# Five chained attentions on one core: key copies issued by GpSimd instead of SyncE, and fewer, wider products in the local attention

## What is computed

```
x = L0(x, ctx)   # masked self-attention, layer norm, masked cross-attention, layer norm, MLP, layer norm
x = L1(x, ctx)   # qn + attention(qn, layer_norm(ctx))
x = L2(x, ctx)   # local attention: key j is kept when i - 64 <= j < i + 65; one key head for all 16 query heads; gate, RMS norm
x = L3(x, ctx)   # attention on layer-normed inputs, then layer norm and a GELU MLP, two residuals
# every attention: softmax(scale * q k^T + mask) v
```

## Time and profile before

| | |
|---|---|
| time of three runs | 2371.82 us median (2369.3 to 2372.09) |
| span of the profiled execution | 2371.4 us |
| mean granted TensorE clock | 0.983 |
| busy: PE, PEld, DVE, ACT, POOL | 94%, 71%, 68%, 64%, 22% |

### The profile page before, as it was taken

One profiled execution on the slowest core, in us unless ns is written; L12 is line 12 of the kernel. 1 busy time (PEld: TensorE's weight loads), 2 busy tenths in 40 slices (PEclk: granted clock), 3 DMA queues, 4 the chain that ended last, 5 costly groups with the idle time before them and its releaser, 6 DMA issues.

```text
span 2371.4 us, 50835 instructions
## 1 busy us (share of the span) xinstructions
PE 2233.3 (94%) x18354; PEld 1675.2 (71%) x18354; DVE 1604.2 (68%) x3312; ACT 1509.9 (64%) x3167; POOL 527.9 (22%) x1120
## 2 busy tenths in 40 slices
PE   6999999999999999999999999999999999999966
PEld 3677777777776676877867677777778686776654
DVE  6768586776767577586675777677756767586422
ACT  5665756777565667658565777566676764766532
POOL 4311122331112132121212332121332212122100
PEclk9999999999999999999999999999999999999977
DMA  7512222331312133113022332112322321122100
GB/s 213 151 47 64 64 60 69 96 93 35 80 37 53 47 99 87 46 52 92 21 66 70 91 82 65 51 45 70 88 61 68 83 60 42 51 61 55 45 7 19
DMA packets 164247, 159.22 MB, mean 67 GB/s; under 512 B 17824, under 2 KB 162720, under 8 KB 162976
## 3 DMA queue, kind: packets, MB, share of 16 engines
q1 hardware_dynamic: 164000, 155.97, 24.0%
HBM read 35.71 MB, written 4.19 MB: 17 GB/s over the span
## 4 chain that ended last, share of the span: by engine, by line
PE 55%; issue 20%; DVE 10%; ACT 5%; POOL 3%; POOLq 2%; DVEq 2%; DMA 1%; SPq 1%; ACTq 0%
PE work L1147 14%; PE work L1138 11%; PE unit L1211 6%; PE unit L1182 5%; PE out L1235 5%; DVE neg_max L1026 5%; PE unit L1207 3%; PE work L1129 2%; ACT unit L792 2%; ACT probs L807 2%; PE unit L1202 2%; PE work L1351 2%; POOL resid L662 1%; DMA query_stack<-max_rows 1%; POOL rstd L652 1%
## 5 line engine op out<-in xcount | busy, mean ns | idle before, releaser
L1026 DVE TENSOR_REDUCE neg_max<-unit 128x2 f32<-128x512 f32 (+1 forms) x1280 | 766.5, 653 | 229.5 <-PE unit L1182 223.3
L807 ACT ACTIVATE probs<-unit 128x512 f32<-128x512 f32 (+1 forms) x1280 | 643.7, 580 | 254.8 <-PE unit L1211 251.9
L1147 PE MATMUL work<-par,hidden_t 128*128 128x256 f32 x1792 | 419.6, 384 | 6.9 <-ACT hidden_t L743 5.8
L1147 PEld LDWEIGHTS work<-par,hidden_t 128*128 128x128 f32 x1792 | 333.1, 191 | 58.0 <-ACT hidden_t L743 9.2
L1182 PE MATMUL unit<-key_stack,query_stack 96*128 96x256 bf16 x2048 | 321.6, 277 | 43.8 <-DMA query_stack<-query_pieces 10.4
L1211 PE MATMUL unit<-query_stack,key_stack 99*128 99x256 bf16 x2048 | 347.6, 275 | 6.9 <-DMA query_stack<-max_rows 3.6
L1138 PE MATMUL work<-tok_t,par 128*128 128x256 f32 x1408 | 339.2, 388 | 3.6 <-ACT tok_t L743 2.5
L1138 PEld LDWEIGHTS work<-tok_t,par 128*128 128x128 f32 x1408 | 260.7, 193 | 44.0 <-ACT tok_t L743 7.2
L1182 PEld LDWEIGHTS unit<-key_stack,query_stack 96*128 96x128 bf16 x2048 | 174.3, 98 | 160.3 <-ACT unit L792 57.0
L1235 PE MATMUL out<-probs,values 128*17 128x256 f32 x4096 | 258.4, 383 | 3.6 <-ACT hidden_t L818 3.4
L1211 PEld LDWEIGHTS unit<-query_stack,key_stack 99*128 99x128 bf16 x2048 | 191.7, 98 | 73.5 <-ACT probs L807 17.5
(11 more groups left out here) (164 smaller groups left out, 3235.8 us busy)
## 6 DMA issues: line engine op xcount, KB each, us to landing
query_stack<-query_pieces SPq DMA_DIRECT2D x480, 128.0 KB, 2.4
key_stack<-key_pieces SPq DMA_DIRECT2D x384, 128.0 KB, 2.4
tok_t<-in_x_features SPq DMA_DIRECT2D x16, 256.0 KB, 2.8
m_in<-in_mask_self SPq DMA_DIRECT2D x16, 256.0 KB, 3.0
x_in<-in_x SPq DMA_DIRECT2D x16, 256.0 KB, 3.0
c_in<-in_ctx SPq DMA_DIRECT2D x16, 256.0 KB, 2.9
ctx_t<-in_ctx_features SPq DMA_DIRECT2D x16, 256.0 KB, 2.9
m_in<-in_mask_cross SPq DMA_DIRECT2D x16, 256.0 KB, 3.1
```

Source lines behind the costliest of these rows:

```text
L807: a_.activation(probs[:, n % PROB_BUFS, k, :, 0:width(l)], bank[:, :, 0:width(l)], ACT.Exp, scale=SCALE[l]).then_inc(exped, 1)
L1026: v.tensor_reduce(neg_max[:, n % HALVES, t, 2 * (u % 4):2 * (u % 4) + 2], bank[:, :, 0:width(l)], AX.X, ALU.max, negate=True).then_inc(max ...
L1147: last = pe.matmul(bank[:, t, :], src[:, t * P:(t + 1) * P], weight, start=(n == 0), stop=(n == len(parts) - 1))
```

## The change

1. **Key copies.** ksplit's six DMAs become steps kcopy0, kcopy1 and kcopy2 (three, two and one DMAs) that POOL issues in its own order; qsplit's become qcopy steps, which stay on SP. The waits are the same ones, now on POOL's queue: for ACT's high piece and for the attention that last used the stack, then for each of DVE's two lower pieces. 480 DMAs move (384 of 128 KB, 96 of 8 KB).
2. **Flag-setting products.** `bits_read` looks up who next uses the bank. If it is a unit that PE starts itself, the flags are of no use and the 128-column product is left out. 18 of 256 remain.
3. **exp products of l2.** The two products of 192 columns become one of 384, since both heads share their weights.
4. **Small buffers.** The norms' moments rotate over 12 places and no longer 4 (`stats` over 2, `sumsq` and `var_eps` over 4), without new waits. The table that says which units ACT primes is written per unit now; all its entries are 1, as before.

The order string is new, but the instructions of DVE and ACT come in the same sequence as before, and those of PE too, except for the products that are gone or merged. On POOL, besides the inserted DMAs, one pair of norm instructions has another place. The core of the diff:

```
+        def copies(eng, key):
+            b, l, step = key
+            keys, piece = step[0] == "k", int(step[-1])
...
+            if piece == 0:
+                if last:
+                    eng.wait_ge(weighed, WEIGH_NO.upto(last + ("weigh3",)))
+                eng.wait_ge(high, no.upto(cut))
+            else:
+                eng.wait_ge(low, 2 * no.upto(cut) - (2 - piece))
+            for at, which in enumerate(rows):
+                if which != piece:
+                    continue
+                dst = stack_[at:ROWS:len(rows), :, :]
+                if keys and l == "l2":
+                    eng.dma_start(dst[:, 0, :], pieces[0:HD, piece, 0, :]).then_inc(placed, 16)
+                else:
+                    eng.dma_start(dst.rearrange("d h n -> d (h n)"),
+                                 pieces[:, piece].rearrange("p c n -> p (c n)")).then_inc(placed, 16)
...
-                    if step in ("ksplit", "qsplit"):
-                        split(key)
+                    if step[:5] == "qcopy":
+                        copies(sp, key)
...
+                    if step[:5] == "kcopy":
+                        copies(pool, key)
...
+        def bits_read(key, half):
+            n = T * UNIT_NO.place[key] + half
+            for m in range(n + UNIT_BUFS, T * len(UNIT_NO.keys), UNIT_BUFS):
+                b, l, step = UNIT_NO.keys[m // T]
+                of_prime = step[:3] in ("pre", "prx")
+                if l != "l2" or not of_prime:
+                    return of_prime
+            return False
...
-                        set_bits(bank[:, :, n:S], S - n)
+                        if bits_read(key, k):
+                            set_bits(bank[:, :, n:S], S - n)
...
-                    for i in range(2):
+                    if l == "l2":
+                        last = pe.matmul(bank[:, :, 0:n], keys[0:MAX_ROWS, 0, k * P:(k + 1) * P],
+                                         queries[0:MAX_ROWS, 2 * u:2 * u + 2, columns(l, k)],
+                                         start=False, stop=True, skip_group_check=True)
+                    for i in range(2 if l != "l2" else 0):
```

More of the change, by code:

```diff
@@ L164 @@
[L164 to L176 removed]
+    "0AA1AsAA0000s00000s1111BBQAA0Q0Q0Q1B011110QA0Q00sQ0Qs00AAAAA00000A0B00s0000s0BR1sR1R10R11sB0AR0001R1"
@@ new lines, with prime_steps, primes @@
+    "fffffPPPPfffdffffefffeffdefeedfffeefedfefefdffeeeedffdfeeddddfffefffffedefffeefeffefffffedeeffeffPPP"
+    "PPffffffffefffeffefeffeefffffefeleflflflfflflleffflefffffffffeffffffffffffffffffffffffffffffffffffff"
+    "fffffffffffffffffffffffff"
+)
+LANES = "0123456789abcdefABCDEFGHIJKLMNOPsQRSTUVWXYZghijkl"
+def prime_steps():
+    return [tuple(step.split(".")) for step in PRIMES.split()]
+def primes(b, l, step):
+    row = PRIMED.get((l, step[:3]))
+    return row is not None and row.split()[b][int(step[3:])] == "1"
@@ new lines, in runs @@
+def runs(key):
+    b, l, step = key
+    if step[:3] in ("pre", "prx"):
+        return primes(b, l, {"pre": "max", "prx": "exp"}[step[:3]] + step[3:])
+    return True
+def schedule():
+    lanes = [(b, steps) for steps in (chain_steps(), beside_steps()) for b in range(B)]
+    lanes += [(B, [("setup", step) for step in SETUP_STEPS])]
+    lanes += [(b, prime_steps()) for b in range(B)]
+    left = {c: (b, iter(steps)) for c, (b, steps) in zip(LANES, lanes)}
+    return [key for key in [(left[c][0],) + next(left[c][1]) for c in ORDER] if runs(key)]
@@ L207, with __init__ @@
 class Numbers:
-    def __init__(self, chosen):
-        self.keys = [k for k in SCHEDULE if chosen(k[1], k[2])]
+    def __init__(self, chosen, also=lambda key: True):
+        self.keys = [k for k in SCHEDULE if chosen(k[1], k[2]) and also(k)]
         self.place = {k: n for n, k in enumerate(self.keys)}
@@ L224 @@
 WORK_NO = Numbers(lambda l, step: step in THROUGH_WORK)
-UNIT_NO = Numbers(lambda l, step: step[:3] in ("pre", "prx") or step[:3] == "max" and l not in PRIMED_MAX
-                  or step[:3] == "exp" and l not in PRIMED_EXP)
+UNIT_NO = Numbers(lambda l, step: step[:3] in ("pre", "prx", "max", "exp"),
+                  lambda key: primer(key) is None)
+FIRST_MASKED = {}
+for _key in UNIT_NO.keys:
+    if _key[2][:3] == "max":
+        FIRST_MASKED.setdefault(_key[:2], _key)
 PRIME_NO = Numbers(lambda l, step: step[:3] in ("pre", "prx"))
@@ L504, in wait_folded @@
                 eng.wait_ge(folded, FOLD_NO.upto((B, "setup", step)))
+        def copies(eng, key):
+            b, l, step = key
+            keys, piece = step[0] == "k", int(step[-1])
+            pieces, stack_, rows = ((key_pieces, key_buffer(b, l), KEY_PIECES) if keys
+                                    else (query_pieces, query_buffer(b, l), QUERY_PIECES))
+            high, low, placed, no = ((key_high, key_low, keys_placed, KSPLIT_NO) if keys
+                                     else (query_high, query_low, queries_placed, QSPLIT_NO))
+            cut = (b, l, "ksplit" if keys else "qsplit")
+            if keys and l == "l2":
+                last = (b - SLOTS, "l2") if b >= SLOTS else None
+            elif keys:
+                last = attention_before(KEY_NO, cut, KEY_STACKS)
+            else:
+                last = attention_before(QSPLIT_NO, cut, QUERY_STACKS)
+            if piece == 0:
[8 more added lines that the diff above has]
+                dst = stack_[at:ROWS:len(rows), :, :]
+                if keys and l == "l2":
+                    eng.dma_start(dst[:, 0, :], pieces[0:HD, piece, 0, :]).then_inc(placed, 16)
+                else:
+                    eng.dma_start(dst.rearrange("d h n -> d (h n)"),
+                                 pieces[:, piece].rearrange("p c n -> p (c n)")).then_inc(placed, 16)
         block = stack.enter_context(nc.Block())
@@ L1086, in run @@
                     elif step == "rms":
-                        n = NORM_NO.place[key]
                         gate, gate_in, diff = quarter(b, l, 3), quarter(b, l, 2), quarter(b, l, 1)
@@ L1099, in run @@
                             last = v.tensor_tensor_reduce(gate[:, t, :], norm[s][:, t, :], norm[s][:, t, :], 1.0, 0.0,
-                                                          ALU.mult, ALU.add, sumsq[:, n % MOMENTS, t:t + 1])
+                                                          ALU.mult, ALU.add, sumsq[:, RMS_NO.place[key] % ROOTS, t:t + 1])
                         last.then_inc(stats_ready, 1)
```

180 lines of the change are left out of this document (82 added, 98 removed), and 36 rows, old and new, of the table CHAIN.

## The result

The changed kernel takes 2507.99 us (median of 4 runs, 2500.01 to 2518.23), the kernel before, run beside it on the same chip, 2371.95 us (2369.3 to 2375.98): a ratio of 1.0566, with a 95% interval of 1.0548 to 1.0585. It is 136 us slower. The prediction was 33 us slower, and even its range ended at 2455.

A forecast was written before the change was run, and what follows sets the result against it. PE, busy 94% of the span, was taken to bound the kernel. The terms -9 (PE) - 3 (SP) + 3.6 (start) + 41 (lateness) gave +33 on 2371.4: 2404 us, 1.4% slower, range 2361 to 2455.

The forecast's parts named there:

- PE's term: PE's shorter stream from fewer flag products and merged exp products: 9 us gained, between 0 and 13.8.
- The price of one copy: POOL's time per key-copy DMA issue: 0.8 us taken, 384 us more on POOL for 480 copies.
- Its bound from above: Highest price of one POOL copy issue: 2.4 us, if POOL were held until the copy lands.
- Lateness, undamped: Results behind copies in POOL's order come late: 33 results, 82 us at 0.8 us per issue, if nothing is won back.
- The replay of POOL's order: All 480 issues followed through POOL's new order: 16 us late at 0.05 us per issue, 49 at 0.6, 82 at 0.8.
- I take half: DVE and ACT work ahead while PE waits, so half the 82 us of lateness counts: 41 us.
- The start: First key copies stand behind POOL's memset, so PE starts at 24.1 us instead of 20.54: 3.6 us lost.
- SP relieved: Maximum-row copies no longer wait behind key copies in SP's queue: 3 us gained (0 to 10).
- DVE's casts shut out by POOL's descriptor writing: Up to 80 casts of `low` could wait one issue each, 64 us of DVE at most; nothing added, range widened.
- the issues are dear: Rival: issues of 1.2 us or more, stretched by DVE's casts: 2454 us at 1.2, about 2500 at 1.5; 12%.
- what would show it: Signs: POOL issues 0.7 to 1.0 us, `max_pieces` waits 50 us or more, longer root waits, start near 24, exp units every 0.33.

The follow-up runs named there:

- the last two steps of the table: Without drains, descriptor space 1024 bytes and two remainder buffers instead of 3072 and one: 2444.5 to 2479.9 us; then drains instead of semaphores (the changed kernel): 2508.0 us.
- the third step: Real POOL copies without drains, 3072 bytes of descriptor space, against SP issuing all copies and POOL running memsets in their places: 2413.1 to 2444.5 us.
- waits alone: Changed kernel, but SP issues all 480 copies and POOL at their places only waits for the same semaphores: 2376.87 us, ratio 1.0023.
- the kernel with memsets: Kernel where SP issues all copies and POOL only waits, plus a 128x512 POOL memset in place of each issue, one remainder buffer: 2413.09 us, ratio 1.0174.
- the kernel with semaphores: Changed kernel with POOL's drains in the cuts and roots replaced by waits on its own semaphore: 2479.88 us, ratio 1.045.

## Why the prediction was wrong

Its direction was right, and PE's term too: 13.8 us as the upper bound, almost all of it for 238 flag products at 0.055 us, 9.0 measured (5.7 to 12), the merged product nothing that can be told. That it took just 9 out of 0 to 13.8 is a choice that no row gave, and its match is luck. The time was 104 us too low. By its steps:

- *The price of one copy.* "Together 0.8 us" for an issue: the row says 0.53. Its bound from above, 2.4 us "if POOL were held until it lands", was named and then not weighed. This is the step that failed. Both ends happen: the issue is as cheap as SP's, and POOL is held until the landing. In the changed kernel itself the drains do it, for 76 us of POOL's time in 35 places, beside 4 issues with 8 us; with the drains gone the descriptor space does it, after every seventh large copy. What the sum lacks is this hold: 63 us by the last two steps of the table, up to 95 if the third step is of the same kind. The kernel's text showed where to look: `g.drain()` stands behind each step of a cut, and the builder's line gives the descriptor space.
- *Lateness, undamped.* The replay of POOL's order came out near in size. It gave 16 us with issues that cost nothing and 49 at 0.6 us; measured are 13 to 15 with waits alone and 13 + 36 = 49 with memsets of 0.54 us and a semaphore each. The second match is partly luck, as the next step shows.
- *"While PE stands, DVE and ACT work off what PE would have waited for next ... I take half."* In idle time something like it is seen: 49 us by the replay, 29 us more idle time of PE in the kernel with memsets. But the lower clock added 20 us of busy time, and so the total was 49 again. As a forecast of time the half failed; the term for the clock was missing.
- *The start.* 3.6 us by a landing of 2.4 us at a quiet time; 9.6 us on the chip, since the copies share the DMA engines with SP's loads once they come after them. The kernel with SP's copies there got 7 us back.
- *SP relieved*, 3 us: PEld's wait for maximum rows went from 10.5 to 9.2 us, and moving the copies in SP's order or off it shows no gain. At most 1 us.
- *DVE's casts shut out by POOL's descriptor writing*, for which nothing was added: the cast of the key's remainder takes 486 ns in the changed kernel and 504 before. The Trainium skill ("SBUF — State Buffer", "Who interferes with whom") counts descriptor writing among what a DVE copy and GpSimd shut each other out for; this trace doesn't bear that out at a size that counts. In the records 45 of the 64 casts ran while POOL issued copies and computed nothing: they took 436 ns on average and 519 at most, against 430 alone, and no large issue took over 775. Memsets in the issues' place do show the lock: 566 ns on average over the 64, some fifteen of them 620 to 720.

Of the rivals "the issues are dear", with 12%, has the right total (about 2500 at 1.5 us) for the wrong reason: no issue of the 384 took over 0.78 us.

Of "what would show it", the waits for `max_pieces` grew past 50 us (the forecast had added PE's and PEld's rows, 29 us before and 189 after, which overlap) and DVE's waits for roots from 31 to 56 us (sums of four rows); exp units came every 0.33 us. The issue rows of 0.7 to 1.0 us and PE's start near 24 us did not come.

The Trainium skill ("DMA: Bandwidth & Descriptors", "SWDGE vs HWDGE vs iDMA") says that GpSimd appends the descriptors of its transfers to rings in a part of SBUF set aside. The runs fit this, and show what the size is worth: with 1024 bytes of a partition the holds come 7 large copies apart (or a multiple) and with 3072 bytes 21, each until all copies in flight have landed.

## What to carry to other kernels

Moving a transfer to GpSimd costs its queue little for the issue and much for what follows: look for a drain behind it and at the descriptor space before counting nanoseconds. Having few transfers in flight doesn't protect against the second: count how many are issued since the last drain, not how many are open. An engine that is idle 78% of the time can be the one that can't take a microsecond more, if its results are taken by the bound engine the moment they are ready; price what stands behind the moved work, not its share of busy time. And where a busy TensorE comes to wait, add what its lower clock costs: here about one microsecond for every two of idle time (45 for 94, and 20 for 29 with memsets). The version that beats both kernels leaves the copies on SyncE and takes PE's edits alone: 2361.7 us, 0.4% faster.

## What the runs showed of the hardware

- A drain on GpSimd behind its own DMA issues ends about 0.3 us after the last of them has landed (35 places of the changed kernel); without the drain GpSimd computes while they fly (at 74 us of the kernel with semaphores).
- GpSimd's issue of a copy of 128 KB takes 0.53 us, nearly without spread (530/530/775 ns), against 545/600/1791 on SyncE; landing 2.7 against 2.4 us. DVE's casts beside such issues were not slowed (436 ns against 430).
- After seven 128 KB copies with 1024 bytes of descriptor space, after 21 with 3072, GpSimd holds its next issue until all copies in flight have landed, though they were only one to four, and starts it 0.4 us later (about 0.6 with the larger space). If none is in flight there is no hold, and a drain in between starts the count anew (all four holds of the changed kernel stand seven copies behind a drain, small ones counted as above). The profile shows this as idle time put down to "issue".
